# Conditional feed-forward kernel: the rank columns of two token tiles turned by one matmul, in-place output, and the head of the load queue in another order

## The reference, cut to what matters

```python
hidden_i  = x @ wi.T                                              # 256 -> 1024
hidden_i += 2 * (x @ common_wi_a.T) @ common_wi_b.T
hidden_i += 2 * (x @ experts_wi_a[id].T) @ experts_wi_b[id].T
hidden_i  = relu(hidden_i)
hidden_o  = hidden_i @ wo.T                                       # 1024 -> 256
hidden_o += 2 * (hidden_i @ common_wo_a.T) @ common_wo_b.T
hidden_o += 2 * (hidden_i @ experts_wo_a[id].T) @ experts_wo_b[id].T
x = x + hidden_o
```

## Time and profile before

| what | us |
|---|---|
| median of three runs | 121.5 |
| the profiled execution, its own time | 121.4 |
| the profiled span | 119.6 |
| PE (matmuls) busy | 114.3 |
| DVE busy | 58.4 |
| ACT busy | 47.6 |
| POOL busy | 41.0 |

### The profile page before, as it was taken

How to read it: one execution, slowest core, us unless ns; L and a number is a source line. 1 busy time by engine, 2 the same in 40 slices (tenths; PEclk the granted TensorE clock), 3 DMA queues, 4 the chain that set the end, 5 groups by cost and what they waited for, 6 DMA issues and landing times.

```text
span 119.6 us, 1980 instructions
## 1 busy us (share of the span) xinstructions
PE 114.3 (96%) x728; PEld 105.0 (88%) x728; DVE 58.4 (49%) x104; ACT 47.6 (40%) x94; POOL 41.0 (34%) x60
## 2 busy tenths in 40 slices
PE   6799999979999999999999999999999999999991
PEld 6678889858889999988889999988889999999990
DVE  4681879699966241125336244325336035526121
ACT  4554619934983321123773324123333103323100
POOL 2032178999989420207375004707000020000000
DMA  3997989999685016114100015114200001111121
GB/s 86 368 257 242 300 270 384 366 370 321 164 248 221 5 35 193 38 47 153 66 5 0 0 36 146 40 49 127 92 0 0 0 9 40 44 44 44 44 93 44
DMA packets 8748, 14.93 MB, mean 125 GB/s; under 512 B 1042, under 2 KB 5138, under 8 KB 8738
## 3 DMA queue, kind: packets, MB, share of 16 engines
q1 hardware_dynamic: 8018, 13.49, 35.2%
q10 hardware_dynamic: 720, 1.31, 3.2%
HBM read 12.70 MB, written 2.10 MB: 124 GB/s over the span
## 4 chain that ended last, share of the span: by engine, by line
PE 87%; POOL 4%; ACT 3%; DMA 3%; DVE 0%; issue 0%; POOLq 0%
PE bank_o L732 36%; PE bank_h L627 30%; PE bank_o L728 5%; PE bank_h L661 5%; PE bank_o L627 5%; POOL b_stack L276 4%; DMA x_raw<-in_x_t 3%; PE bank_low L678 2%; ACT hid L379 2%; PE bank_o L751 1%; PE bank_low L627 1%; PE bank_h L704 1%; ACT b_stack L367 1%; PE bank_o L742 1%; ACT xT L357 1%; PE bank_o L693 0%
## 5 line engine op out<-in xcount | busy, mean ns | idle before, releaser
L732 PE MATMUL bank_o<-wcat,hid 128*128 128x272 f32 x336 | 45.1, 289 | 0.0
L732 PEld LDWEIGHTS bank_o<-wcat,hid 128*128 128x128 f32 x336 | 43.4, 188 | 0.0
L627 PE MATMUL bank_h<-xT,wiT 128*128 128x512 f32 x156 | 41.6, 410 | 0.7 <-ACT xT L357 0.7
L627 PEld LDWEIGHTS bank_h<-xT,wiT 128*128 128x128 f32 x156 | 29.6, 199 | 6.5 <-ACT xT L357 1.0
L475 DVE SCALAR_TENSOR_TENSOR hid<-bank_h,hid 128x512 fp32r<-128x512 f32 x26 | 17.3, 687 | 14.1 <-ACT hid L379 14.1
L379 ACT ACTIVATE hid<-bank_h 128x512 fp32r<-128x512 f32 x26 | 14.8, 597 | 18.8 <-PE bank_h L661 18.5
L552 DVE TENSOR_TENSOR o_sb<-bank_o,x_nat 128x256 f32<-128x256 f32 x16 | 6.7, 423 | 19.3 <-PE bank_o L751 17.2
L276 POOL TENSOR_TENSOR b_stack<-b_raw,b_stack 32x1024 fp32r<-32x1024 f32 x6 | 14.3, 2391 | 3.9 <-ACT b_stack L367 3.8
L661 PEld LDWEIGHTS bank_h<-low_stack,b_stack 128*128 128x128 f32 x52 | 8.7, 189 | 2.4 <-DVE low_stack L475 1.0
L267 POOL CAST a_stack<-a_raw 128x192 fp32r<-128x192 f32 x8 | 3.4, 421 | 20.5 <-DMA a_raw<-in_rec_a 20.5
L402 ACT ACTIVATE rank_sb<-bank_o 128x64 fp32r<-128x64 f32 x14 | 3.2, 225 | 18.0 <-PE bank_o L732 18.0
(11 more groups left out here) (58 smaller groups left out, 105.5 us busy)
## 6 DMA issues: line engine op xcount, KB each, us to landing
b_raw<-in_rec_b SPq DMA_DIRECT2D x8, 512.0 KB, 4.8
x_nat<-in_x_n SPq DMA_DIRECT2D x4, 512.0 KB, 5.8
out<-o_sb SPq DMA_DIRECT2D x16, 128.0 KB, 1.7
x_raw<-in_x_t SPq DMA_DIRECT2D x6, 256.0 KB, 3.0
w_raw<-in_wo_t SPq DMA_DIRECT2D x4, 256.0 KB, 5.4
w_raw<-in_wi_t ACTq DMA_DIRECT2D x3, 256.0 KB, 4.5
a_raw<-in_rec_a SPq DMA_DIRECT2D x8, 96.0 KB, 2.8
bo_raw<-in_rec_bo SPq DMA_DIRECT2D x8, 96.0 KB, 4.0
```

The costliest lines, as they stand in the source:

```text
L627: nc.tensor.matmul(up_bank(q, m)[:, :], wiT_at(sw, k, m), xT[q % 2][sx][:, k, :], start=start, stop=False)
L732: last = nc.tensor.matmul(bank_o[g % NO][:, 0:WIN], hid[q % 2][sh][:, m, tok], wcat[sw][:, m, win], start=(m == 0 and i == 0), stop=(m == ...
```

## The change

Seven edits, in the code's own terms:

- `turn` is run for two token tiles at a time. `rank_sb` has three parts (high, high, low) of 2 x 16 columns, one half for each tile of the pair; one matmul turns both. `bo_stack` is made twice as wide: the first 256 columns have the expert's factor in the rows of the first tile and zeros in those of the second, the other 256 columns the reverse. The host lays these rows out, so that each load of Bo has twice the bytes. There are still 14 `fin`; there are 7 `turn` for 14.
- In `down` tiles 0 and 1 are turned in the middle of tile 2, with their two `fin` at the end of tile 2; tiles 2 and 3 are turned where tile 3 was, with both `fin` in the next stage. `own_wo_product(0)` and `(1)` come after tile 0 of down 2.
- There are four `bank_o` and three `bank_h`; each token tile has its own bank. From step 2 on, hidden tiles 3 and 4 use `bank_o0` and `bank_o1`.
- `add` writes into `x_nat` in place of `o_sb`, and a new `x_nat` is loaded only when all four stores of the step before last have landed.
- `WARM_UP` is 7.
- On SP the ids are loaded first, before `wi`; only the registers that are needed next are loaded from them, and the last four of them after `wo`. On ACT the casts of B of step 1 come after hidden tiles 1 and 3 in place of 3 and 5.
- The loads of A and Bo of step 3 are issued behind the last store of down 0 and the load of `x_nat` of step 2.

The diff, cut to its core:

```diff
-    WARM_UP = 6
-    NO = 3
+    WARM_UP = 7
+    NO = 4
+    NH = 3
...
-            return bank_h[m % 4]
+            return (bank_h + bank_o[0:2] + bank_h)[m]
...
-        bo_stack = [sb(f"bo_stack{i}", [KT, PAIR, D], F32R) for i in range(2)]
+        bo_stack = [sb(f"bo_stack{i}", [KT, PAIR, 2 * D], F32R) for i in range(2)]
...
             def load_x_nat(q):
                 if q >= 2:
-                    sp.wait_ge(added, (q - 1) * TT)
+                    for t in range(TT):
+                        sp.wait_ge(stored[t], (q - 1) * 16)
...
+            sp.dma_start(idt[:, :], ids.rearrange("(o n) -> o n", o=1)).then_inc(ids_in, 16)
             for k in range(KD):
                 sp.dma_start(w_raw[:, 0, k * 2 * P:(k + 1) * 2 * P], wi_t[0][:, k * 2 * P:(k + 1) * 2 * P]).then_inc(wi0_in[k], 16)
-                if k == 0:
-                    sp.dma_start(idt[:, :], ids.rearrange("(o n) -> o n", o=1)).then_inc(ids_in, 16)
...
-                if 1 <= q and q + 2 < STEPS:
-                    for b in range(PAIR):
-                        load_a(q + 2, b)
-                    load_bo(q + 2)
                 for t in range(1, TT):
                     store(q, t)
                 if q + 2 < STEPS:
                     load_x_nat(q + 2)
+                if q + 3 < STEPS:
+                    for b in range(PAIR):
+                        load_a(q + 3, b)
+                    load_bo(q + 3)
...
                     hidden_hi(0, m)
-                    if m in (3, 5):
-                        split_b_hi(1, m // 2 - 1)
+                    if m in (1, 3):
+                        split_b_hi(1, m // 2)
...
-                nc.vector.tensor_tensor(o_sb[:, t, :], bank_o[g % NO][:, at:at + D], x_nat[q % 2][:, t, :],
+                nc.vector.tensor_tensor(x_nat[q % 2][:, t, :], bank_o[t][:, at:at + D], x_nat[q % 2][:, t, :],
                                         ALU.add).then_inc(added, 1)
...
-                pe.wait_ge(rank_lo, g + 1)
-                nc.tensor.matmul(bank_o[g % NO][0:KT, TURN_AT:], rank_sb[g % 2][:, :, :].rearrange("p i r -> p (i r)"),
+                pe.wait_ge(rank_lo, 2 * (pair + 1))
+                nc.tensor.matmul(bank_o[t][0:KT, TURN_AT:], rank_sb[pair % 2][:, :, :, :].rearrange("p i s r -> p (i s r)"),
                                  ident[:, :], start=False, stop=True, skip_group_check=True).then_inc(turn_done, 1)
...
                 down_main(q, 0, SECOND_HALF)
                 if before is not None:
-                    fin(before, TT - 1)
-                for t in range(1, TT):
-                    down_main(q, t, FIRST_HALF)
-                    if not own_wo(q * TT + t - 1):
-                        turn(q, t - 1)
-                    if q == STEPS - 2:
-                        own_wo_product(t - 1)
-                    down_main(q, t, SECOND_HALF)
-                    if not own_wo(q * TT + t - 1):
-                        fin(q, t - 1)
+                    fin(before, 2)
+                    fin(before, 3)
+                if q == 2:
+                    own_wo_product(0)
+                    own_wo_product(1)
+                down_main(q, 1)
+                down_main(q, 2, FIRST_HALF)
+                turn(q, 1)
+                if q == 2:
+                    own_wo_product(2)
+                down_main(q, 2, SECOND_HALF)
+                fin(q, 0)
+                fin(q, 1)
+                down_main(q, 3)
                 if q + 2 < STEPS:
                     ranks_in(q + 2, 0)
                     ranks_in(q + 2, 1)
-                    turn(q, TT - 1)
+                    turn(q, 3)
                     up_main(q + 2, 0)
```

More of the change, by code:

```diff
@@ L56, in sem @@
             return ctx.enter_context(nc.semaphore(name))
-        bank_h = [ctx.enter_context(nc.psum_tensor(f"bank_h{i}", [P, BANK], F32)) for i in range(4)]
+        bank_h = [ctx.enter_context(nc.psum_tensor(f"bank_h{i}", [P, BANK], F32)) for i in range(NH)]
         bank_o = [ctx.enter_context(nc.psum_tensor(f"bank_o{i}", [P, BANK], F32)) for i in range(NO)]
@@ L74, in up_bank_free @@
         def up_bank_free(q, m):
-            if q == 0:
+            if q == 0 or (q > 1 and m in (3, 4)):
                 return 0
@@ L212, in _ @@
             load_b(0)
-            expert += [sp.value_load(idt[0:1, n:n + 1], min_val=0, max_val=E - 1) for n in range(PAIR, B)]
             load_x(1)
-            for b in range(PAIR):
-                load_a(1, b)
+            for n in range(PAIR):
+                expert.append(sp.value_load(idt[0:1, PAIR + n:PAIR + n + 1], min_val=0, max_val=E - 1))
+                load_a(1, n)
             sp.wait_ge(common_zero, 1)
@@ L226, in _ @@
                 sp.dma_start(w_raw[:, i, :], wo_t[i]).then_inc(wo_in[i], 16)
+            expert += [sp.value_load(idt[0:1, n:n + 1], min_val=0, max_val=E - 1) for n in range(2 * PAIR, B)]
             load_bo(0)
@@ L595, in down @@
                         split_x_lo(q + 2, k)
-                for t in range(1, TT):
-                    if q == 2:
-                        own_wo_sum(t - 1)
-                    if q == 3 and t == 1:
-                        own_wo_sum(3)
-                        own_wo_lo(3)
-                    add(q, t - 1)
-                    if not own_wo(q * TT + t):
-                        ranks_lo(q, t)
-                    if q == 1 and t == 2:
-                        last_ao_part_lo()
-                    if q == 2:
-                        own_wo_lo(t - 1)
+                if q == 3:
+                    own_wo_sum(3)
+                    own_wo_lo(3)
+                ranks_lo(q, 1)
+                if q == 2:
+                    own_wo_sum(0)
+                    own_wo_sum(1)
+                    own_wo_lo(0)
+                add(q, 0)
+                add(q, 1)
+                if q == 1:
+                    last_ao_part_lo()
+                if q == 2:
+                    own_wo_lo(1)
+                if q < STEPS - 1:
+                    ranks_lo(q, 2)
+                    if q == 2:
+                        own_wo_sum(2)
+                        own_wo_lo(2)
+                    ranks_lo(q, 3)
                 if q + 2 < STEPS:
                     ranks_in_lo(q + 2)
-                add(q, TT - 1)
+                add(q, 2)
+                add(q, 3)
             for what, q in STAGES:
@@ L631, in up_main @@
                     pe.wait_ge(hid_lo, up_bank_free(q, m))
+                elif q > 1:
+                    pe.wait_ge(added, (q - 2) * TT + m - NH + 1)
                 if up_bank(q, m) is ranks_bank(q):
@@ L692, in wo_product @@
                     m = 2 * i + jj
[L693 removed]
+                    last = nc.tensor.matmul(bank_o[2 + i % 2][:, jj * D:(jj + 1) * D], common_st[:, m * P:(m + 1) * P],
                                             common_st[:, F:], start=True, stop=True)
@@ L703, in own_wo_product @@
                     m = 2 * i + jj
-                    last = nc.tensor.matmul(bank_h[i][:, jj * D:(jj + 1) * D], common_st[:, m * P:(m + 1) * P],
-                                            bo_stack[(STEPS - 1) % 2][:, PAIR - 1, :], start=True, stop=True)
+                    last = nc.tensor.matmul(own_bank(i)[:, jj * D:(jj + 1) * D], common_st[:, m * P:(m + 1) * P],
+                                            bo_stack[(STEPS - 1) % 2][:, PAIR - 1, 0:D], start=True, stop=True)
                 last.then_inc(prod_done, 1)
@@ L790, in up @@
                     if m == 1:
+                        fin(before, TT - 2)
                         fin(before, TT - 1)
```

95 lines of the change are left out of this document (48 added, 47 removed).

## The result

The changed kernel took 120.57 us (median of four runs, 119.40 to 121.89); the kernel before took 121.42 beside it. The ratio is 0.989, with a 95% interval of 0.985 to 0.993: faster by 0.7 to 1.5%. The same file run again, six times, gave 120.00 us (119.75 to 120.39), ratio 0.988 (0.986 to 0.991). The profiled execution took 121.05 us with a span of 119.3, against 121.4 and 119.6 before.

A forecast was written before the change was run, and what follows sets the result against it. The prediction took PE to be the bound, busy 114.3 of 119.6 us. From 121.4 us it subtracted 0.77 for turns and 0.27 for a wait, giving 120.4, with an 8-in-10 range of 118.5 to 121.0.

The forecast's parts named there:

- Seven turns fewer, 0.77: PE's chain in all four steps: each removed turn saves 0.11 us, seven save 0.77, bounds 0.42 to 0.84.
- Bo twice as wide at cost 0: POOL's operations on Bo: 2.5 us more a step, covered by later waits, so cost 0.
- Its own alarm: A PE wait over 0.3 us behind 30 us, or a first product after 4.8 us, would make the prediction wrong.
- The wait in front of `up_lora(1,0)`, -0.27, handed to DVE: PE's wait at 26.02: B comes earlier, `low_stack` then holds PE until 25.75; gain 0.27 us, not 0.83.
- The failed step: POOL's subtractions for B of step 1 end at about 24.9, if its common-factor work is done by then.
- The warm-up's seventh matmul, gain 0: Before the first product: it takes about 0.45 us inside 0.71 us of idle time, delays nothing, gains 0.
- The first rival: Start of PE: a shorter idle break lets the clock rise earlier, saving 1.6 us, time 118.8; chance 0.36.
- fewer than eleven cold matmuls are left: Start of PE: eleven matmuls should still take 4.85 us; fewer would mean the clock rises earlier.
- Ids first at cost 0: Start: `wi` is issued 0.33 to 0.38 us later, its cast still ends before ACT's cast of x; cost 0.
- Its condition: Ahead of the first product, x and not `wi` must come last for loading ids first to cost 0.
- The third rival, B of step 1 late for ACT,: ACT's in-order queue waits for B of step 1, landing after 20.0; PE late, about 123 us; chance 0.06.

The follow-up runs named there:

- second profile: The changed kernel, unedited, run again and profiled a second time; that execution took 119.75 us, the median of the runs was 120.00 us.
- seven zeros: The kernel before with WARM_UP 7 in place of 6 and nothing else changed; 121.98 us, ratio 0.999.
- the head alone: The kernel before with WARM_UP 7, ids first, and the change's register loads and casts of B of step 1, turns one by one; 119.82 us, ratio 0.986.
- the head with cover: The kernel before with the change's start and two tiles' products ahead of the first needing B of step 1, turns one by one; 118.62 us, ratio 0.976.
- POOL's other order: The change with POOL's split of Bo of step 1 moved behind a copy of A, so B of step 2 is split sooner; 120.88 us, ratio 0.984.
- six zeros: The change with WARM_UP 6 in place of 7; 120.49 us, ratio 0.989.
- common factors first: The change with the common factors loaded ahead of x and A of step 1 and split ahead of A on POOL; 120.84 us, ratio 0.993.
- the turns alone: The change with WARM_UP, ids, register loads and casts of B of step 1 as in the kernel before; 121.55 us, ratio 0.999.
- with cover: The change with products of two more tiles put ahead of the first that needs B of step 1; 119.15 us, ratio 0.981.
- last-but-one experiment: The change with Bo's split later and two products ahead of B of step 1, plus DVE's common-factor work behind the fourth hid split; 121.64 us, ratio 0.988.
- the best kernel: The change with POOL's split of Bo of step 1 later and two products ahead of the one needing B of step 1; 118.43 us, ratio 0.974.

## Why the prediction was right, and where it was not

The forecast of 120.4 lay within 0.2 of the first median and 0.4 above the second. Its sum was -0.77 - 0.27. By the second profile the true one is -0.78 (turns) + 0.50 (76.85 - 76.35, the slow splits and the wait at a turn) - 1.36 (the head) = -1.64, against the 121.40 - 119.75 = 1.65 of the executions. That the total came close was luck: a missed loss hid part of a missed gain, and late loads hid more of it in some executions.

*Seven turns fewer, 0.77: right.* The body is 77.13 us in all four kernels profiled with single turns (before, seven zeros, the head alone, the head with cover), and 76.35 in all four with paired turns and POOL's other order (to 0.01 each). The difference is 0.78, seven times 0.111. The Trainium skill's 55.6 ns a matmul (TensorE: Matmul & The Clock Gate, "Wait — 56ns, not 53.3ns?") would have made it an estimated 0.39. The measurement is twice that: as the prediction read from its rows, the half tile behind a turn is longer too. In the profile with POOL's other order the first matmul behind `turn(0,1)` alone carries it: it takes 0.34 us and starts its successor after 0.18, its neighbours 0.29 and 0.12. Its weights were loaded from the turn's start on, 0.06 us ahead of it, the next one's 0.12 ahead; that this is the cause was not tested. Behind a `fin`, which has another shape as well, no half tile is longer.

*Bo twice as wide at cost 0: wrong, 0.48 us.* POOL's two operations on Bo took 15.8 us in the change's first profile and 10.1 before, 1.4 a step more where the prediction had 2.5. I looked for who waits for POOL, and found cover. POOL's later split of B of step 2 is indeed waited for by nobody. But it moved from 35.58 to 38.74, to beside DVE's splits of x, and slowed them. How far depends on the head: with POOL's order unchanged the body was 76.40 (six zeros), 76.56 (common factors first: 114.37 - 37.81), 76.83 to 76.85 (the change and the turns alone) and 77.18 (with cover), against 76.35. The prediction had asked what is late next, and not what runs beside it. Its own alarm, a wait of PE of over 0.3 us behind 30 us, just misses it in the first profile (0.28) and just catches it in the second (0.31), where the body lost 0.48 and 0.50, so the length of a stretch says more than the list of waits.

*The wait in front of `up_lora(1,0)`, -0.27, handed to DVE: half right.* It was handed to `low_stack` in the second profile, but with PE going on at 24.64 instead of 25.75, since all behind it moves with the earlier pace. In the first profile it stayed POOL's. The failed step is "POOL's work on the common factors is out of the way; that depends on a load which SP now issues over 2 us earlier": A of step 1 was issued at 8.10 in one execution and used by POOL at 15.52, in the other issued at 8.40 and used at 13.57. An earlier issue was read as an earlier landing.

*The warm-up's seventh matmul, gain 0: right in itself, wrong as a forecast of the head.* The first rival named the effect, and its sign that fewer than eleven cold matmuls are left came true. Neither edit is needed for it by itself: with six zeros and ids first the pace was fast at once, and with seven and ids late at 5.96. The rival's cause, the shorter break, is not shown, and not refuted: ahead of the first product PE stood idle for 0.52 to 0.71 us in the three profiles with the late rise, that of before among them, and for 0.36 or less in the eleven others. In the thirteen changed kernels' profiles the fast pace came at 9.4 to 10.7 where neither was done, and otherwise between 4.3 and 7.3. What decides within that range was not settled: with six zeros and 0.34 us of idle time the fast pace came at 4.33, in the change's first profile, with none listed, at 7.04. Ids first makes the first product start sooner, by 0.36 and 0.12 us in the change's two profiles, and so makes the break shorter.

*Ids first at cost 0: not quite.* Its condition was that x and not `wi` comes last. In the second profile the first product waited 0.17 us for DVE's split of `wi`; in the first it waited for neither.

*The third rival, B of step 1 late for ACT,* did not come: ACT waited 0.19 us for it in the first profile, at 17.93, and not at all in the second. The late load was A, which POOL waits for.

## What to carry to other kernels

Before an operation of POOL is lengthened or moved, list what DVE does beside it in its new place, not only who waits for it. An earlier pace of PE is a gain only as far as the next operand is earlier too: give PE independent products there, and check two profiles, since loads scatter. Divide the span into a head that scatters and a body; where no wait in the body hangs on the head, a gain of 0.78 us that medians of six runs cannot show stands there to the hundredth.

## What was not expected of the hardware

- DVE beside POOL. The split of x takes 0.69 us, and two of them 3.80 beside POOL's split of B; POOL's two subtractions went from 4.71 to 5.20 there. The scaling of 96x256 rows took 0.29 us in the kernel before and 2.16 in the last-but-one experiment; it has one SBUF input, and why it took so long there is not shown. The splits of hid, which read PSUM and one SBUF operand, kept to 0.63 each (three in 1.89) beside POOL. The split of the 32x256 common rows shows a pattern: it ended 0.28 us behind POOL's subtraction in the best kernel (16.11 + 2.57 = 18.68 against 16.01 + 2.39 = 18.40), 0.28 behind it with `common_b` later (24.34 against 24.06), and 0.27 behind POOL's cast in the kernel before (18.42 against 18.15; timelines of DVE and POOL):

```profile
17.28 1.14 DVE L475 SCALAR_TENSOR_TENSOR common_st<-common_raw,common_st 32x256 fp32r<-32x256 f32 x1
```

```profile
17.06 1.09 POOL L301 CAST common_st<-common_raw 96x1024 fp32r<-96x1024 f32 x1
```

  This reads as a wait for POOL's instruction to end and some 0.28 behind it, not as a slower pace. The second split of x fits: it ended at 44.49, 0.55 behind POOL's second subtraction (38.74 + 5.20 = 43.94). The Trainium skill says so (SBUF — State Buffer, "Who interferes with whom"): a DVE instruction with two SBUF inputs contends with a GpSimd instruction that reads SBUF, and the second to come waits for the first. The trace agrees.
- After PE had stood for 1.94 and for 3.15 us, the granted clock fell to 0.50, the 1.2 GHz level, for some 3 us and for over 5. After the change's own 2.10 us it stayed at 1.00 in the profiled execution.
